# Attention and feed-forward block: rows moved between partitions by four copies inside SBUF instead of a trip over DRAM, and three edits of order

## What is computed

```python
mod = (silu(c) @ wmod).reshape(4, 6, 1, 512)      # sa, ca, ga, sb, cb, gb
h = layernorm(x) * (1 + ca) + sa
q, k = h @ Wq.T, h @ Wk.T                         # 64 features
p = softmax(q @ k.T)                              # the same scores for all 16 heads
x1 = x + ga * ((p @ (h @ Wv.T)) @ Wo.T)           # ga, gb: absolute value at least 0.25
h2 = layernorm(x1) * (1 + cb) + sb
out = x1 + gb * (sum_r(h2 @ factors[r]) / sqrt(8) + bias)
```

## Time and profile before

| | us |
|---|---|
| median of 3 runs | 449.67 |
| lowest, highest | 448.71, 452.26 |
| the profiled execution, its own time | 449.63 |
| its span in the profile | 447.8 |
| TensorE busy (matmuls) | 439.6 (98%) |
| VectorE busy | 356.6 (80%) |
| ScalarE busy | 320.0 (71%) |
| GpSimd busy | 234.9 (52%) |
| bytes moved by DMA | 88.05 MB |

### The profile page before, as it was taken

How to read it: one execution, slowest core, us unless ns; L and a number is a source line. 1 busy time by engine, 2 the same in 40 slices (tenths; PEclk the granted TensorE clock), 3 DMA queues, 4 the chain that set the end, 5 groups by cost and what they waited for, 6 DMA issues and landing times.

```text
span 447.8 us, 7294 instructions
## 1 busy us (share of the span) xinstructions
PE 439.6 (98%) x2118; PEld 361.6 (81%) x2118; DVE 356.6 (80%) x610; ACT 320.0 (71%) x642; POOL 234.9 (52%) x308
## 2 busy tenths in 40 slices
PE   8899999999999999999999999999999999999996
PEld 7586888878888888788888888888888888887885
DVE  5787557868887887988897878888886777999977
ACT  3677557778797786678877787779777664667651
POOL 0554516852555643356565544456564527177982
PEclk9999999999999999999999999999999999999999
DMA  8999986533665457667676367766686146658423
GB/s 308 393 388 287 256 156 115 120 121 108 204 210 184 133 159 217 205 210 235 209 243 201 117 200 221 234 187 215 187 254 198 47 140 203 200 172 278 131 79 141
DMA packets 77750, 88.05 MB, mean 197 GB/s; under 512 B 5000, under 2 KB 55944, under 8 KB 77200
## 3 DMA queue, kind: packets, MB, share of 16 engines
q1 hardware_dynamic: 73872, 80.51, 56.4%
q0 software_dynamic: 3264, 6.29, 7.9%
q10 hardware_dynamic: 576, 0.79, 0.5%
HBM read 53.49 MB, written 34.10 MB: 196 GB/s over the span
## 4 chain that ended last, share of the span: by engine, by line
PE 77%; DVE 9%; issue 4%; POOL 3%; ACT 3%; DMA 3%; SPq 0%; DVEq 0%; POOLq 0%; ACTq 0%
PE ps_o L525 9%; PE ps_o L527 9%; PE ps_o L526 9%; PE ps_v L525 5%; PE ps_v L526 5%; PE ps_v L527 5%; PE ps_y L525 4%; PE ps_y L527 4%; PE ps_y L526 4%; PE ps_qk L525 3%; PE ps_qk L526 3%; PE ps_qk L527 3%; PE ps_s L614 2%; PE ps_s L615 2%; PE ps_t L531 1%
## 5 line engine op out<-in xcount | busy, mean ns | idle before, releaser
L1685 POOL TENSOR_SCALAR ve<-mv 128x1 f32<-128x1 f32 x64 | 17.0, 266 | 160.0 <-DVE mv L1320 119.3
L525 PE MATMUL ps_o<-v_lo,pt_hi 128*128 128x512 f32 x192 | 74.9, 390 | 1.0 <-DVE pt_lo L1205 0.9
L526 PE MATMUL ps_o<-v_hi,pt_lo 128*128 128x512 f32 x192 | 74.8, 389 | 0.0
L527 PE MATMUL ps_o<-v_hi,pt_hi 128*128 128x512 f32 x192 | 74.8, 389 | 0.0
L1205 DVE TENSOR_TENSOR h_lo<-h_f,h_hi 128x512 fp32r<-128x512 f32 x57 | 41.6, 730 | 29.0 <-ACT h_hi L843 28.7
L871 ACT ACTIVATE h_f<-x1b,mod_t 128x128 f32<-128x128 f32 x120 | 52.9, 594 | 3.8 <-DVE x1b L1338 3.8
L1687 POOL TENSOR_TENSOR rstd<-ve,minus_half 128x1 f32<-128x1 f32 x64 | 45.8, 716 | 5.3
L525 PEld LDWEIGHTS ps_o<-v_lo,pt_hi 128*128 128x128 f32 x192 | 36.0, 188 | 9.3 <-issue 1.8
L525 PE MATMUL ps_v<-wvo_lo,h_hi 128*128 128x512 f32 x108 | 43.1, 399 | 0.3 <-DVE h_lo L1205 0.3
L919 ACT ACTIVATE probs<-ps_s,negmax 128x1024 f32<-128x1024 f32 x32 | 35.4, 1108 | 10.0 <-DVE negmax L1264 9.7
L526 PE MATMUL ps_v<-wvo_hi,h_lo 128*128 128x512 f32 x108 | 42.2, 391 | 0.0
(11 more groups left out here) (238 smaller groups left out, 1193.2 us busy)
## 6 DMA issues: line engine op xcount, KB each, us to landing
x_blocks<-xn SPq DMA_DIRECT2D x50, 256.0 KB, 2.8
p_blocks<-probs SPq DMA_DIRECT2D x24, 512.0 KB, 3.8
pb<-p_blocks SPq DMA_DIRECT2D x96, 128.0 KB, 2.7
x1b<-x_blocks SPq DMA_DIRECT2D x30, 256.0 KB, 2.8
result<-x_ring SPq DMA_DIRECT2D x15, 512.0 KB, 3.0
xb<-x_blocks SPq DMA_DIRECT2D x20, 256.0 KB, 3.0
x_ring<-in_x SPq DMA_DIRECT2D x18, 256.0 KB, 4.0
wmod<-in_wmod SPq DMA_DIRECT2D x4, 1024.0 KB, 14.9
```

Of the source, the lines that this page charges most:

```text
L525: nc.tensor.matmul(acc, a_hi, b_lo, start=first, stop=False)
L526: nc.tensor.matmul(acc, a_lo, b_hi, start=False, stop=False)
L527: return nc.tensor.matmul(acc, a_hi, b_hi, start=False, stop=last)
L1685: nc.gpsimd.tensor_scalar(ve[:, one], mv[:, u, 1:2], EPS, None, ALU.add).then_inc(ve_done, 1)
```

## The change

- The three DRAM buffers go. `to_blocks` issues four transfers from SBUF to SBUF, one for each group of 32 partitions; `move_x`, `move_x1` and `move_p` each take the place of a send and a fetch.
- Because a partition now receives four neighbouring rows of the probabilities too, `in_quarters` reads and writes them as `(c b)`, in steps of four floats.
- Waits on `x2n_out`, `xn_out`, `p_out` become waits on `x1b_loaded`, `xb_loaded`, `pb_loaded`: `xn` and `probs` are free when all four copies have landed.
- SP's order in `step` and in the tail is drawn together: the move of the probabilities comes before that of x.
- VectorE's prologue: `h_first(0)` and `h_second(0)` come ahead of `moments_of(2)`, and with that ahead of `wvo_rest(0)`.
- GpSimd: `of_x(12)` comes after two of the four rests of the factors instead of after all four.

```diff
         def in_quarters(tile):
-            return tile.rearrange("p k (b c) -> p k b c", b=Q)
+            return tile.rearrange("p k (c b) -> p k b c", b=Q)
...
-            def blocks_out(blocks, rows, done, count, out_sem):
-                wait_alone(sp, sp_passed, done, count)
-                sp.dma_start(blocks.rearrange("a p x -> p a x"),
-                             rows[:].rearrange("p (a x) -> p a x", a=Q)).then_inc(out_sem, 16)
-            def blocks_in(to, blocks, loaded):
-                sp.dma_start(to[:], blocks.rearrange("a (c b) x -> (a c) (b x)", b=Q)).then_inc(loaded, 16)
...
+            def to_blocks(to, rows, loaded):
+                for a in range(Q):
+                    sp.dma_start(to[BLK * a:BLK * (a + 1), :], rows[:, P * a:P * (a + 1)]).then_inc(loaded, 16)
+
+            def move_x(q):
+                wait_alone(sp, sp_passed, xn_done, q + 1)
                 wait_alone(sp, sp_passed, h_f_done, q)
-                blocks_in(xb, x_blocks[u], xb_loaded)
+                to_blocks(xb, xn, xb_loaded)
+
+            def move_x1(t):
+                wait_alone(sp, sp_passed, x2n_done, t + 1)
+                if t > 0:
                     wait_alone(sp, sp_passed, h2_f_done, t)
-                blocks_in(x1b, x1_blocks[u], x1b_loaded)
+                to_blocks(x1b, xn, x1b_loaded)
+
+            def move_p(t):
                 n = trips_of(t)
                 sp.wait_ge(exp_done, t + 1)
-                if n > 1:
-                    sp.wait_ge(pb_loaded, 16 * Q * (n - 1))
-                sp.dma_start(p_blocks[n & 1].rearrange("a p x -> p a x"),
-                             probs[:].rearrange("p (a x) -> p a x", a=Q)).then_inc(p_out, 16)
-
-            def fetch_p(t):
-                n = trips_of(t)
-                sp.wait_ge(p_out, 16 * (n + 1))
                 sp.wait_ge(pt_lo_done, 2 * (t - 1))
                 for a in range(Q):
-                    sp.dma_start(pb[BLK * a:BLK * (a + 1), n & 1, :].rearrange("c (b x) -> c b x", b=Q),
-                                 p_blocks[n & 1, a].rearrange("(b c) x -> c b x", b=Q)).then_inc(pb_loaded, 16)
+                    sp.dma_start(pb[BLK * a:BLK * (a + 1), n & 1, :],
+                                 probs[:, KEYS // Q * a:KEYS // Q * (a + 1)]).then_inc(pb_loaded, 16)
...
             def step(t):
                 opening = scored_last_in(t - 1)
-                if 12 <= t + TB + 1 < T:
-                    fetch_x(t + TB + 1, 1 - u)
                 if opening is not None:
-                    send_p(opening)
-                if t + 1 < T and not turned_by_pe(t + 1):
-                    fetch_p(t + 1)
+                    move_p(opening)
                 if 1 <= t < T - 1:
-                    send_x1(t - 1, 1 - u)
+                    move_x1(t - 1)
                 if u and g >= 2:
                     store_pair(g - 2)
-                if 1 <= t < T - 1:
-                    fetch_x1(t - 1, 1 - u)
...
+                if scored_in(t) is not None and not turned_by_pe(scored_in(t)):
+                    move_p(scored_in(t))
                 if 12 <= t + TB + 2 < T:
-                    send_x(t + TB + 2, u)
-                if scored_in(t) is not None and not turned_by_pe(scored_in(t)):
-                    send_p(scored_in(t))
+                    move_x(t + TB + 2)
...
+            move_p(25)
+            move_p(26)
+            move_x1(23)
+            move_p(27)
+            move_x1(24)
+            move_p(28)
+            move_p(29)
+            move_x1(25)
+            move_x1(26)
+            move_p(30)
             store_pair(10)
+            move_p(31)
+            move_x1(27)
             store_pair(11)
+            move_x1(28)
+            move_x1(29)
...
             def normalize_x_blocks(q, u):
                 act.wait_ge(nmr1_done, q + 1)
-                act.wait_ge(x2n_out, 16 * (q - TB - 2))
+                act.wait_ge(x1b_loaded, 16 * Q * (q - TB - 2))
...
-                    act.wait_ge(p_out, 16 * trips_of(t))
+                    act.wait_ge(pb_loaded, 16 * Q * trips_of(t))
...
                 elif after_x:
-                    act.wait_ge(xn_out, 16 * (t - 1))
+                    act.wait_ge(xb_loaded, 16 * Q * (t - 1))
                 else:
-                    act.wait_ge(x2n_out, 16 * t)
+                    act.wait_ge(x1b_loaded, 16 * Q * t)
...
+            h_first(0)
+            h_second(0)
             moments_of(2)
-            h_first(0)
             wvo_rest(0)
-            h_second(0)
...
             pool.wait_ge(bias_loaded, 16)
-            for k in range(C):
-                pool.wait_ge(f_hi_done, k + 1)
-                nc.gpsimd.tensor_tensor(f_lo[:, k, :], f_sum[:, k, :], full(f_hi[:, k, :]),
-                                        ALU.subtract).then_inc(f_lo_done, 1)
+            factor_rest(0)
+            factor_rest(1)
             of_x(TB + 4, 0)
+            factor_rest(2)
+            factor_rest(3)
```

More of the change, by code:

```diff
@@ L258, in adaln_block @@
             sem(n) for n in ("x2n_done", "h2_ps", "h2_f_done", "h2_hi_done", "h2_lo_done"))
-        xn_out, xb_loaded, xb_turned = sem("xn_out"), sem("xb_loaded"), sem("xb_turned")
-        x2n_out, x1b_loaded, x1b_turned = sem("x2n_out"), sem("x1b_loaded"), sem("x1b_turned")
+        xb_loaded, xb_turned = sem("xb_loaded"), sem("xb_turned")
+        x1b_loaded, x1b_turned = sem("x1b_loaded"), sem("x1b_turned")
         y_acc, ffn_done, biased_done, gated_done, y_done = sem("y_acc"), sem("ffn_done"), sem("biased_done"), sem("gated_done"), sem("y_done")
@@ L453, in step @@
                 opening = scored_last_in(t - 1)
-                if 12 <= t + TB + 1 < T:
-                    fetch_x(t + TB + 1, 1 - u)
                 if opening is not None:
-                    send_p(opening)
-                if t + 1 < T and not turned_by_pe(t + 1):
-                    fetch_p(t + 1)
+                    move_p(opening)
                 if 1 <= t < T - 1:
-                    send_x1(t - 1, 1 - u)
+                    move_x1(t - 1)
                 if u and g >= 2:
                     store_pair(g - 2)
-                if 1 <= t < T - 1:
-                    fetch_x1(t - 1, 1 - u)
-                if t < T - TB and t % TB in (2, 4):
+                if t % TB in (2, 4):
                     spread_gate(t % TB // 2 - 1, t // TB + 1)
+                if scored_in(t) is not None and not turned_by_pe(scored_in(t)):
+                    move_p(scored_in(t))
                 if 12 <= t + TB + 2 < T:
-                    send_x(t + TB + 2, u)
-                if scored_in(t) is not None and not turned_by_pe(scored_in(t)):
-                    send_p(scored_in(t))
+                    move_x(t + TB + 2)
                 if 2 * TB <= t + TB + 3 < T and t >= 5:
@@ L940, in normalize_x1 @@
                     act.wait_ge(xt_ps, TB + 3 + t)
-                    wait(act, x2n_out, 16 * t)
+                    wait(act, x1b_loaded, 16 * Q * t)
                 elif after_x:
-                    act.wait_ge(xn_out, 16 * (t - 1))
+                    act.wait_ge(xb_loaded, 16 * Q * (t - 1))
                 else:
-                    act.wait_ge(x2n_out, 16 * t)
+                    act.wait_ge(x1b_loaded, 16 * Q * t)
                 nc.scalar.activation(blocked(xn), in_blocks(x_ring[:, t & (2 * TB - 1), :]), ACT.Identity,
@@ L1331, in turn_x @@
             def turn_x(q):
-                dve.wait_ge(xb_loaded, 16 * (q - TB - 3))
+                dve.wait_ge(xb_loaded, 16 * Q * (q - TB - 3))
                 nc.vector.transpose(xb[:], xb[:]).then_inc(xb_turned, 1)
             def turn_x1(t):
-                dve.wait_ge(x1b_loaded, 16 * (t + 1))
+                dve.wait_ge(x1b_loaded, 16 * Q * (t + 1))
                 nc.vector.transpose(x1b[:], x1b[:]).then_inc(x1b_turned, 1)
@@ L1414, in gate_next_to_last @@
             def gate_next_to_last():
-                dve.wait_ge(p_out, 16 * trips_of(T))
+                dve.wait_ge(pb_loaded, 16 * Q * trips_of(T))
                 dve.wait_ge(y_acc, 31)
@@ L1768, in sum_factors, with factor_rest @@
                 nc.gpsimd.tensor_tensor(f_sum[:, k, :], f_sum[:, k, :], g_sum[:, k, :], ALU.add).then_inc(f_summed, 1)
+            def factor_rest(k):
+                pool.wait_ge(f_hi_done, k + 1)
+                nc.gpsimd.tensor_tensor(f_lo[:, k, :], f_sum[:, k, :], full(f_hi[:, k, :]),
+                                        ALU.subtract).then_inc(f_lo_done, 1)
             def last_wv_rest():
```

43 lines of the change are left out of this document (1 added, 42 removed).

## The result

The changed kernel takes 468.99 us (median of 4 runs, 467.17 to 471.52) against 449.42 us (4 runs, 448.71 to 452.26): ratio 1.043, 95% interval 1.040 to 1.047. It is slower, as forecast, but by 19.6 us and not by 7.8, and outside the range of 447.5 to 461.5.

The account below looks back on a forecast made before the run. TensorE was taken to bound the kernel, with VectorE close behind in the tail. 449.6 - 0.9 - 0.45 + 1.0 + 4.6 + 3.5 = 457.4 us, range 447.5 to 461.5.

Parts of the forecast that it names:

- Part 4, the price of a step: Turned probabilities in steps of four floats: each 512-element instruction takes 0.45 us longer, on ScalarE and VectorE alike.
- the two rivals in which VectorE pays nothing or half: Steps of four floats: only ScalarE pays, 449.3 us, chance 0.25; or VectorE pays 0.22 us each, 452.8 us, chance 0.15.
- the one in which the tail is freed: Tiles 26 to 31: the shorter hop frees the tail if VectorE pays under 0.05 us per step; 448.0 us, chance 0.07.
- Part 4, the tail: Tail, up to tile 30's first `pt_lo`: 11 longer VectorE instructions, less 0.3 us slack, lose 4.6 us.
- Part 4, the loop: Loop over tiles: VectorE's 0.9 us more in odd steps reaches TensorE; a loss of 3.5 us, ends 0 and 5.6.
- The discount from 5.6 to 3.5: Loop: earlier landing of x and longer waits of VectorE for TensorE give part of 5.6 us back, leaving 3.5.
- Part 3, the wait that takes its place: `xn` free only once `x1b` has landed: loses 0 in the loop and 1.0 us in the tail, ends 0 and 3.
- The fourth rival: Loop: the small copies land after 5.5 us instead of 4.1, so ScalarE waits for `xn`; 462 us, chance 0.05.
- 1.6 us more of a queue that is idle most of a step of 12 us, so 0: Loop: SP's eight small copies per tile instead of four larger add 1.6 us to its queue and cost 0.
- Part 3, the gain: First VectorE-turned tile of a batch: one hop removes VectorE's 2.04 us wait and TensorE's 0.45 us; gain 0.45, ends 0 and 1.5.
- Part 2: Before tile 3's attention: tile 12's moments ahead of two factor rests remove the 0.87 us wait; gain 0.9, ends 0 and 1.0.
- Part 1: Prologue: tile 0's rest ahead of tile 2's moments only moves TensorE's gap; gain 0, ends 0 and 0.9.

Follow-up runs that it names:

- k_again: The changed kernel run once more without any edit; 469.73 us (2 runs), ratio 1.045.
- after: The changed kernel itself in its first profiled execution, against the kernel before; 468.99 us, ratio 1.043.
- n_steps: l_both with one edit reversed, so the turned probabilities are again in steps of four floats; 460.74 us, ratio 1.022.
- e_two: The changed kernel with a second buffer for x1's rows in place of the bias; 462.43 us, ratio 1.028.
- l_both: The changed kernel with runs of 32, second buffer, x1's buffers alternating in the tail, tile 30's probabilities ahead of tile 26's x1; 449.3 us.
- b_steps: The kernel before with only the steps of four floats added, transfers still over DRAM; 463.6 us, ratio 1.032.
- f_tworuns: The changed kernel with runs of 32 floats and a second buffer for x1's rows in place of the bias; 453.11 us, ratio 1.007.
- b_factor: The kernel before with only tile 12's moments moved ahead of two of the factors' rests; 449.53 us, ratio 0.999.
- d_pmove: The changed kernel with x and x1 over DRAM again; probabilities still by four copies in steps of four floats; 473.1 us, ratio 1.049.
- a_runs: The changed kernel with the turned probabilities in runs of 32 floats again, the four copies kept; 464.89 us, ratio 1.033.
- b_order: The kernel before with both edits of order (prologue and factors' rests) and nothing else; 451.15 us, ratio 1.002.
- g_xfirst: a_runs, one buffer, with x's copies issued ahead of the probabilities' copies in each step; 461.99 us, ratio 1.025.
- run 10: Not a label of a run: the text reads "At the start of the run 10 matmuls", a count of matmuls in the changed kernel's first execution.

## Why the prediction was wrong

The changed kernel's 20.4 us on TensorE (21.0 in `k_again`), by stretch, beside the terms of the forecast:

| stretch | forecast | measured, `after` and `k_again` | of it the steps (`n_steps`, same stretch) |
|---|---|---|---|
| start, before matmul 60 | 0 | 2.6 and 0.7 | 1.1, varies by execution |
| prologue, 60 to 480 | 0 | 0.4 and 0.4 | 0.3 |
| around tile 3, 480 to 600 | -0.9 | 2.7 and 1.3 | -0.5 |
| loop, 600 to 1680 | 3.5 - 0.45 | 7.3 and 10.5 | 6.3 (3.3 in `e_two`) |
| tail, 1680 to the end | 4.6 + 1.0 | 7.4 and 8.1 | 5.0 |

**Part 4, the price of a step: right.** 0.45 us per instruction was forecast for both engines; ScalarE pays 0.495 and VectorE 0.41 by medians. So the two rivals in which VectorE pays nothing or half are ruled out, and so is the one in which the tail is freed. The Trainium skill's rule ("SBUF — State Buffer", "Door 1: The DMA port swizzle (why `[64,N]` ≈ `[32,N]`)"), by which VectorE pays as ScalarE does, agrees with these rows.

**Part 4, the tail: right.** 4.6 forecast; 4.4 (`n_steps` less `l_both`) and 5.8 (`b_steps`) measured.

**Part 4, the loop: the term was too small.** "I take 3.5; ends 0 and 5.6": measured 5.8 (`b_steps`), 7.8 (`n_steps` less `l_both`) and 4.8 (`e_two` less `f_tworuns`). All three lie above 3.5, and they are 3.0 apart, so the size is known only roughly. The odd steps lose what was worked out for them (0.8 to 0.9 at matmuls 1140 and 1260 in `n_steps`, for instance), little gives it back, and steps between them lose 0.1 to 0.6 more. The discount from 5.6 to 3.5 rested on "the earlier landing of x and longer waits of VectorE for TensorE", and no row had shown either.

**Part 3, the wait that takes its place: this step failed most.** It was put at 0 in the loop and 1.0 in the tail. Against `n_steps`, which has the steps but neither the shared buffer nor the order in the tail, the changed kernel's median is 8.2 us longer (9.7 by the two ratios, each against the kernel before of its own session). On TensorE the difference is 3.2 or 1.8 us at tile 3 (`after` or `k_again`), 1.0 or 4.2 in the loop and 2.4 or 3.1 in the tail.

The copies' length was not what failed, though by luck: 1.3 us of issuing plus 2.8 of landing were forecast, three further issues take 1.86 and the landing 2.2, and both sums are about 4.1 (94.82 to 98.98 is 4.2). For the probabilities 4.0 was forecast, and 1.86 + 3.5 is 5.4. The fourth rival, x1's copies landing at 5.5 us, is not what happened, although its sign came true: TensorE's gaps at tile 3 and in the tail stand where ScalarE waits for `x1b`. What failed is where the landing is waited for:

- The first tiles were not searched. There a move waits for the modulation before it while x's tile 12 already wants `xn`, and Part 2's gain, which `b_factor` has on TensorE, was swallowed (`e_two` and `d_pmove`, without this wait, have no loss there).
- In the loop the wait for `x1b` was found (0.5 us late was worked out; at line 837 it is 0.2 to 0.5 in nine steps and 1.5 in two). Its mirror image was not: x1's normalization now waits for the copies of x, 9.0 us in 9 waits in `after` and 17.3 in 14 in `k_again`.
- In the tail one wait was followed to its end (it came: 3.66 where 3 was worked out) and allowed to shrink, where three come one behind another (3.66, 1.48, 1.90).
- "1.6 us more of a queue that is idle most of a step of 12 us, so 0" looked at SyncE's load and not at its order. Four issues take 2.48 us, whatever stands behind them is that much later, and what stands in front can be a wait for ScalarE.

That the shared buffer costs less beside the steps than without them is shown by the times (6.9 and 11.7 us, above). Why is my reading of the waits and not shown by a run of its own: ScalarE's wait for `xb` is 32.3 us in `a_runs` and 9.0 or 17.3 in the changed kernel, since ScalarE comes later by its own longer work.

**Part 3, the gain: not there to be had.** VectorE's 2.04 us before the first turn of a batch and the 0.45 at 184.59 went, as forecast, but they cannot be credited to the one hop. In `b_factor`, with the probabilities still over DRAM, that wait is 0.67 and the 0.45 is gone too; in `b_steps` the wait is 0.77. And `l_both`, which has the one hop without the couplings, is as fast as before. The trips over DRAM were hidden.

**Part 2: right** in mechanism and size (0.9 on TensorE in `b_factor`, as forecast), though too small for the times to show. **Part 1:** 0 was taken with ends of 0 and 0.9 of gain; it costs some 0.6 (0.65 at 26.43; 0.3 to 0.8 between matmuls 60 and 480 in the runs that have it, 0.2 and -0.6 in `b_steps` and `b_factor`; 1.6 between the times of `b_order` and `b_factor`). "Only reordered, not less" left out that the work moved had filled a wait.

The direction came out right for the reason that had been given most weight. The range failed at its upper end, because it was built from the doubling of one price and not from the couplings.

No version tried beats both kernels by more than the measurement tells: the kernel before with the factors' rests in the new order is at 0.999 (0.997 to 1.001).

## What to carry to other kernels

In this kernel the trip in two hops was also a buffer: it freed its source when the first hop had landed, whatever held the destination. Before merging such hops, list for each transfer who waits for the source, who holds the destination and what stands behind it in the issuing queue, at the start and in the tail as well as in a steady step. And work moved out of a place may have been filling a wait there: look whose idle time it covered.

## What the runs showed of the hardware that I had not expected

Issuing a copy from SBUF to SBUF took SyncE 0.62 us where the fetch from DRAM into the same 32 partitions took 0.44 (2.48 and 1.75 for four). Copies of 64 KB landed in 2.2 to 2.7 us each (medians of the profiles), those of 128 KB in 3.5, against 2.7 for the fetch of 128 KB from DRAM. For x and x1 the four pieces together took about 4.1 us, where one leg over DRAM with all 256 KB took 2.8 to 3.0. So a set of four copies on chip was no shorter than a leg over DRAM.

The sums of TensorE by stretch (us, busy, matmuls, granted clock, DMA) in the first execution of the changed kernel, then in the second:

```profile
5.00:9.00 4.00, 4.00 (x10) 1.00 1.05 396
105.40:108.70 3.30, 3.30 (x9) 0.51 0.10 30
```

```profile
5.00:9.00 4.00, 4.00 (x16) 1.00 1.04 388
105.40:108.70 3.30, 3.13 (x14) 1.00 0.29 82
```

After TensorE's gap of 1.93 us at 104.18 the granted clock was 0.51 from 105.4 on, the lower of its two levels (1.2 and not 2.4 GHz), which cost about 1.4 us. In the second execution the gap there was 1.75 us and the clock stayed at 1.00. The same fall follows gaps of 2.2 us in `f_tworuns` (0.51 between 417 and 420), 2.4 in `e_two` and 2.5 in `g_xfirst`, but not the gap of 2.51 at 433.81 in the changed kernel. At the lower level the matmuls of 512 columns start 0.43 us apart:

```profile
105.78 0.63 PE L483 MATMUL ps_o<-v_lo,pt_hi 128*128 128x512 f32 x1
106.21 0.63 PE L484 MATMUL ps_o<-v_hi,pt_lo 128*128 128x512 f32 x1
```

At the start of the run 10 matmuls and not 16 start in the same 4 us, in the first execution with this same spacing of 0.43 and duration of 0.63, although the granted clock reads 1.00 in both. It looks like the lower level; the granted clock does not show it, and why it lasts longer in one execution than in the next stays open.
